# Weight splits, first projections and selection moved into the chunk loop, output projections parked in HBM and done between the heads of a mixture-of-depths block on one core

## The reference

```
# branch 1: gated linear attention, 16 heads of 32, in blocks with a decaying state
q, k, v, u = split(xn @ W_qkvu.T);  q, k = silu(q), silu(k)
o = decayed causal attention(q, k, v) ;  o = u * o * rsqrt(mean(o*o) + 1e-6) ;  y1 = o @ W_out.T
# branch 2: mixture of depths: the router takes 256 of the 2048 tokens
scores = xn @ w_router ;  idx = sort(top_k(scores, 256)) ;  s = xn[idx]
h = rms_norm(s, ln1) ;  q = rope(h@wq + bq) (16 heads of 128), k = rope(h@wk + bk), v = h@wv + bv (8 heads)
x1 = s + causal_softmax_attention(q, k, v) @ wo
processed = x1 + (silu(h2@w_gate) * (h2@w_up)) @ w_down        # h2 = rms_norm(x1, ln2)
y2 = xn ;  y2[idx] = gate*processed + (1-gate)*s               # gate = sigmoid(scores[idx])
output = x + y1 + y2
```

## Time and profile before

| what | value |
|---|---|
| time, median of 3 runs | 641.75 us (632.86 to 777.0) |
| the profiled execution's own time | 638.01 us |
| its span, first to last instruction | 636.3 us |
| busy: TensorE, VectorE, GpSimd, ScalarE | 531.2, 367.6, 280.1, 241.2 us |
| mean granted TensorE clock, as a share of full speed | 0.921 |

### The profile page before, as it was taken

How to read it: one execution, slowest core, us unless ns; L and a number is a source line. 1 busy time by engine, 2 the same in 40 slices (tenths; PEclk the granted TensorE clock), 3 DMA queues, 4 the chain that set the end, 5 groups by cost and what they waited for, 6 DMA issues and landing times.

```text
span 636.3 us, 11375 instructions
## 1 busy us (share of the span) xinstructions
PE 531.2 (83%) x4522; PEld 484.2 (76%) x4522; DVE 367.6 (58%) x651; ACT 241.2 (38%) x418; POOL 280.1 (44%) x183
## 2 busy tenths in 40 slices
PE   3989999999999999999993465846679758599993
PEld 3979998998989989998882444835669757499992
DVE  5886455345534554336676646998897986412231
ACT  7632322222322222235776102343544554434430
POOL 4644544354525453533341635535233233538762
PEclk9999999999999999999996676969869878899998
DMA  8420120110011100020012142242310321225522
GB/s 272 158 35 18 36 33 2 35 35 34 2 35 34 34 7 13 18 83 1 20 56 95 34 148 83 67 132 72 127 67 1 133 67 66 66 81 185 188 78 33
DMA packets 24020, 42.70 MB, mean 67 GB/s; under 512 B 4192, under 2 KB 4192, under 8 KB 23840
## 3 DMA queue, kind: packets, MB, share of 16 engines
q1 hardware_dynamic: 23424, 40.67, 19.9%
q0 software_dynamic: 544, 1.31, 1.1%
HBM read 37.25 MB, written 4.73 MB: 66 GB/s over the span
## 4 chain that ended last, share of the span: by engine, by line
PE 60%; DVE 18%; issue 11%; ACT 6%; POOL 3%; DMA 1%; SPq 0%; DVEq 0%; ACTq 0%; POOLq 0%
PE bank L1115 18%; PE bank L1075 7%; PE bank L1076 7%; PE bank L1077 7%; PE bank L1106 5%; PE bank L1129 4%; DVE staged L829 3%; PE bank L1175 3%; PE bank L1165 3%; DVE rope L826 2%; PE bank L1159 2%; ACT marks L405 2%; DVE rope L824 2%; PE bank L1137 1%; PE bank L1085 1%
## 5 line engine op out<-in xcount | busy, mean ns | idle before, releaser
L1015 POOL TENSOR_TENSOR wlo<-raw,whi 128x2048 fp32r<-128x2048 f32 x24 | 110.9, 4621 | 118.9 <-ACT whi L428 118.9
L1115 PE MATMUL bank<-xTh,Wh 128*128 128x256 f32 x384 | 113.1, 294 | 2.4 <-DVE Wl L620 2.1
L1115 PE MATMUL bank<-xTh,Wl 128*128 128x256 f32 x384 | 109.3, 285 | 0.0
L1115 PE MATMUL bank<-xTl,Wh 128*128 128x256 f32 x384 | 109.2, 284 | 0.0
L1115 PEld LDWEIGHTS bank<-xTh,Wh 128*128 128x128 f32 x384 | 74.3, 194 | 3.4 <-DVE xTl L611 2.5
L1075 PE MATMUL bank<-HTh,whi 128*128 128x256 f32 x224 | 66.4, 297 | 10.4 <-DVE staged L817 6.6
L1115 PEld LDWEIGHTS bank<-xTl,Wh 128*128 128x128 f32 x384 | 74.4, 194 | 0.1
L1115 PEld LDWEIGHTS bank<-xTh,Wl 128*128 128x128 f32 x384 | 74.2, 193 | 0.0
L683 DVE TENSOR_TENSOR A<-bank,DEC 128x512 f32<-128x512 f32 x64 | 39.8, 684 | 52.3 <-PE bank L1129 52.3
L992 POOL TENSOR_TENSOR state<-kv_new,state_dec 128x512 f32<-128x512 f32 x15 | 19.4, 1290 | 110.6 <-DVE kv_new L690 110.6
L1076 PE MATMUL bank<-HTl,whi 128*128 128x256 f32 x224 | 65.9, 294 | 0.0
(11 more groups left out here) (211 smaller groups left out, 1375.6 us busy)
## 6 DMA issues: line engine op xcount, KB each, us to landing
XX<-in_x SPq DMA_DIRECT2D x16, 256.0 KB, 3.0
out<-BASE SPq DMA_DIRECT2D x16, 256.0 KB, 2.7
raw<-in_wq SPq DMA_DIRECT2D x4, 1024.0 KB, 5.1
raw<-in_wo SPq DMA_DIRECT2D x4, 1024.0 KB, 5.5
raw<-in_w_gate SPq DMA_DIRECT2D x4, 1024.0 KB, 4.9
...
```

Source lines behind the costliest of these rows:

```text
L1015: Q.tensor_tensor(wlo[b % 3][:], raw[b % 2][:], whi[b % 3][:].bitcast(f32), ALU.subtract)\
L1115: ins = T.matmul(bank[:, half * GROUP:(half + 1) * GROUP], w[:, k, cols], xt[:, g % 2, k, :], start=m % steps == 0, stop=m % steps == step ...
```

## The change

- **Order of the layer norm.** Normed rows are made two tiles per slot (three ahead of the loop), stored to HBM and loaded again for the transposition from tile 3 on. Router scores are complete after slot 4.
- **Ranking and gather.** The 16 comparisons stand in slots 6 to 9, four in each; choice in slot 10, indices and gather in slot 11, norm, split and transposition of the gathered rows in slot 12. The normed rows themselves are gathered, so the second layer norm of the selected rows is gone.
- **Units in the last chunks.** Slots 14 and 15 hold units 0 to 7 in the places of the projection tiles; their weight blocks are split from slot 13 on, two per slot. Units 8 to 15 stand in head steps 0 to 5, 7 and 8. The output weights become a 25th block (`W0`).
- **Output projections.** `uo` of each chunk is stored to HBM. In head step h (2 to 16) it is loaded back and split, in steps 3 to 16 `project_out(h - 3)` runs, ScalarE moves the result out (`evacuate_out`), VectorE adds the reloaded `x` (`final`), and it is stored. Projections 14 and 15 come behind the heads. Two PSUM banks serve units and output projections in turn.
- **Low halves.** GpSimd writes each low half in four instructions of 128x512. The addition `BASE` on GpSimd is gone; the rms power is taken once for all 16 chunks.
- **Addresses.** Every buffer has a fixed address; blocks lie on top of the first branch's weights, which are free by then.

```diff
-                  "D": tall(w_down)}
-        order = ["K0", "K1", "V0", "Q0", "V1", "Q1", "Q2", "O0", "Q3", "O1", "O2", "O3",
+                  "D": tall(w_down), "W": wide(WoT)}
+        order = ["K0", "Q0", "V0", "Q1", "W0", "K1", "Q2", "V1", "O0", "Q3", "O1", "O2", "O3",
...
-        units = [(k, p) for k in ("K0", "K1", "V0", "Q0", "V1", "Q1", "Q2", "Q3") for p in range(2)]
-        before_heads = 10
...
+        units = [(k, p) for k in ("K0", "Q0", "V0", "Q1", "K1", "Q2", "V1", "Q3") for p in range(2)]
+        in_chunks = 8
+        unit_of_step = {0: 8, 1: 9, 2: 10, 3: 11, 4: 12, 5: 13, 7: 14, 8: 15}
+        PT_AT, OUT_AT, PV_AT, WO_AT, FINAL_AT = 2, 3, 3, 4, 4
...
+        bank_jobs = [("unit", u) for u in range(in_chunks)]
+        for h in range(STEPS):
+            bank_jobs += [("unit", unit_of_step[h])] if h in unit_of_step else []
+            bank_jobs += [("out", h - OUT_AT)] if 0 <= h - OUT_AT < late_outs[0] else []
+        bank_jobs += [("out", N) for N in late_outs]
...
-        rank_in = {(N_TILES - 4, 0): (0, 1), (N_TILES - 4, 1): (2, 3), (N_TILES - 4, 2): (4, 5),
-                   (N_TILES - 3, 0): (6, 7), (N_TILES - 3, 1): (8, 9), (N_TILES - 3, 2): (10, 11),
-                   (N_TILES - 2, 0): (12, 13), (N_TILES - 2, 1): (14, 15)}
-
-        split_after = {2: "Q3", 6: "O1", 7: "O2", 10: "O3", 12: "G0", 15: "U0"}
+        hi_after = {0: "Q2", 1: "V1", 2: "O0", 4: "Q3", 6: "O1", 8: "O2", 9: "O3", 12: "G0", 16: "U0"}
+        load_at = {0: "V1", 1: "O0", 2: "Q3", 3: "O1", 5: "O2", 7: "O3", 9: "G0", 10: "U0", 13: "G1", 17: "U1"}
+
+        def ln_tiles(N):
+            return [M for M in (2 * N + 7, 2 * N + 8) if NX <= M < N_TILES]
+
+        RANK, CHOOSE, INDEX, HIDDEN = 6, 10, 11, 12
+
+        def ranked(N, position):
+            return 4 * (N - RANK) + position if RANK <= N < RANK + N_TILES // 4 else None
...
+            def store_xn(M):
+                sp.wait_ge(xn_ok, M + 1)
+                sp.dma_start(xn_t[M], XN[:, M % NX, :]).then_inc(xn_out[M % NX], 16)
+
+            def load_xn(M):
+
+                sp.wait_ge(xn_out[M % NX], 16 * (M // NX + 1))
+                if M >= NX + 2:
+                    sp.wait_ge(xt_ps, M - 1)
+                sp.dma_start(XA[:, M % 2, :], xn_t[M]).then_inc(xa_in[M % 2], 16)
...
+                if N == N_TILES - 4:
                     load_block(0)
                     load_block(1)
-                    sp.wait_ge(counted, N_TILES)
-                    sp.dma_start(bqk[:, 0:FKV], bk).then_inc(part_in, 16)
-                    sp.dma_start(bqk[:, FKV:], bq).then_inc(part_in, 16)
-                    sp.dma_start(ln12[:, 0, :], ln1).then_inc(part_in, 16)
-                    sp.dma_start(ln12[:, 1, :], ln2).then_inc(part_in, 16)
-                    sp.dma_start(bvb[:], bv.partition_broadcast(P)).then_inc(part_in, 16)
+                if N == N_TILES - 3:
                     load_block(2)
-            store(N_TILES - 2)
-            load_block(3)
-            store(N_TILES - 1)
-            for b in range(4, len(order)):
...
+            for h in range(STEPS):
+                if h in load_at:
+                    load_block(block_of[load_at[h]])
+                if 2 <= h - 1 < N_TILES:
+                    load_uo(h - 1)
+                if 2 <= h - OUT_AT < N_TILES:
+                    load_x_again(h - OUT_AT)
+                if 0 <= h - FINAL_AT < late_outs[0]:
+                    store(h - FINAL_AT)
...
+            def split_uo(N):
+                act.wait_ge(ur_in[N % 2], 16 * (N // 2 + 1)), act.wait_ge(uo_lo, N), act.wait_ge(out_ps, N)
+                S.activation(uoh[:], UR[:, N % 2], ACT.Copy).then_inc(uo_hi, 1)
+
+            def evacuate_out(N):
+
+                act.wait_ge(out_ps, N + 1), act.wait_ge(r_ok, 1), act.wait_ge(gains_ok, 1)
...
+            def final(N):
+
+                dve.wait_ge(evac_ok, N + 1), dve.wait_ge(xr_in[N % 2], 16 * (N // 2 + 1)), dve.wait_ge(gains_ok, 1)
+                V.scalar_tensor_tensor(out=XR[:, N % 2, :], in0=XR[:, N % 2, :], scalar=gain[:, N:N + 1],
+                                       in1=evac[:, N % 2, :], op0=ALU.mult, op1=ALU.add).then_inc(final_ok, 1)
...
             def block_lo(b):
                 pool.wait_ge(fw_hi, b + 1)
-                pool.wait_ge(*last_use(b - 3))
-                Q.tensor_tensor(wlo[b % 3][:], raw[b % 2][:], whi[b % 3][:].bitcast(f32), ALU.subtract)\
-                    .then_inc(fw_lo, 1)
-
-            pool.wait_ge(consts, 1)
-            ln_rstd(0, CH)
-            base(0)
-            base(1)
-            ln_rstd(CH, 1)
+                high, low = halves(b)
+                for k in range(4):
+                    ins = Q.tensor_tensor(low[:, k, :], raw[b % 2][:, k, :], high[:, k, :].bitcast(f32), ALU.subtract)
+                ins.then_inc(fw_lo, 1)
...
+                if N >= N_TILES - 3:
+                    block_lo(2 * (N - (N_TILES - 3)))
...
+            for h in range(STEPS):
+                if 0 <= h - 2 < late_outs[1]:
+                    uo_low(h - 2)
+                if h in hi_after:
+                    block_lo(block_of[hi_after[h]])
+            uo_low(late_outs[1])
             rows_rms(1)
...
             def transposed(M):
 
-                pe.wait_ge(xn_ok, M + 1), pe.wait_ge(masks_ok, 1)
+                pe.wait_ge(masks_ok, 1)
+                if M < NX:
+                    pe.wait_ge(xn_ok, M + 1)
+                    rows = XN[:, M, :]
+                else:
+                    pe.wait_ge(xa_in[M % 2], 16 * ((M - NX) // 2 + 1))
+                    rows = XA[:, M % 2, :]
                 if M >= 2:
...
             def project_out(N):
-                pe.wait_ge(uo_hi, N + 1), pe.wait_ge(uo_lo, N + 1), pe.wait_ge(ms_o_ok, N + 1), pe.wait_ge(w_lo, 1)
+                block_ready(block_of["W0"])
+                pe.wait_ge(uo_hi, N + 1), pe.wait_ge(uo_lo, N + 1)
+                bank_free(("out", N))
                 for k in range(NK):
-                    ins = split_matmuls(out_bank[:], (uoh[:, k, :], uol[:, k, :]), (Woh[:, k, :], Wol[:, k, :]),
+                    ins = split_matmuls(job_bank("out", N)[:], (uoh[:, k, :], uol[:, k, :]), (Woh[:, k, :], Wol[:, k, :]),
                                         k == 0, k == NK - 1)
...
+            def bank_free(job):
+
+                n = bank_jobs.index(job) - 2
+                if n < 0:
+                    pe.wait_ge(proj_sb, NPROJ * G + n + 1)
+                elif bank_jobs[n][0] == "out":
+                    pe.wait_ge(evac_ok, bank_jobs[n][1] + 1)
+                else:
...
-                for u in units_of_step.get(h, ()):
-                    unit(u)
-                if h == PV_AT:
-                    pe.wait_ge(unit_lo, before_heads)
+                if h in unit_of_step:
+                    unit(unit_of_step[h])
+                if h == 0:
+                    rms(N_TILES - 1)
...
+                if 0 <= h - OUT_AT < late_outs[0]:
+                    project_out(h - OUT_AT)
```

1148 lines of the change are left out of this document (602 added, 546 removed).

## The result

The changed kernel takes **607.81 us** (median of 4 runs, 604.61 to 608.34) against 641.87 beside it: a ratio of 0.950, 95% interval 0.940 to 0.961. The ratio is one of means, and leaves out one slow run of the kernel before, of 777.0 us. The change is faster and inside the range (548 to 615), but 26 us above the forecast of 582, outside the forecast's own 560 to 600, and nearer to rival 2's 612. The profiled execution took 607.73 us, its span is 605.7.

What follows compares the result with a forecast made beforehand. TensorE was taken to bound the chunk loop, VectorE and GpSimd in turn the units. Chunks 299 + slots 14 and 15 55 + heads 134 + tail 92.7 = 580.7 us span, 1.7 more gives 582; own range 560 to 600, whole range 548 to 615.

Steps and rivals of the forecast that it cites:

- rival 2: Slots 14, 15 and heads: nothing overlaps, latency adds by a factor of 1.21; 64 and 155 us, 612 in all; chance 0.18.
- Chunks, 299: Slots 0 to 13: thirteen output projections leave TensorE, 35.7 us, and 3 + 1 come in; the stage ends at 299 us.
- issued a slot ahead of their use; hidden: Chunk loop: normed rows go over HBM, 2.7 us out and about as much back, at no cost to the path.
- Slots 14 and 15, 55: Slots 14 and 15 with eight units: VectorE 32 plus GpSimd 32 us, less 9 that may overlap, make 55 us.
- Ends: 36 and 64: Limits for slots 14 and 15: 36 us if TensorE alone bounds, 64 if nothing of VectorE and GpSimd overlaps.
- Heads, 134: Heads: 84 us for steps 0 to 9 plus 50 for steps 10 to 19, sum 134; ends 111 and 155.
- I book no gain for it: Heads: cutting a low half into four lets VectorE in after 1.15 us instead of 4.6, but the total stays the same.
- Four low halves per block instead of one change nothing here: Tail: making each low half in four instructions was to cost or gain nothing there.
- Tail, 92.7: Tail: 88.7 us as before plus 4 us for the later rms power of x1, 92.7 us.
- The two late output projections fit in that gap: Tail: the two late output projections, 5.5 us, fit in the 4 us gap ahead of the transpositions.
- Rival 4: Heads: the ring of two banks makes 16 steps cost 12 us each; 662 us in all, slower than before; chance 0.05.
- steps 10 to 15 at 6 us: Heads, a sign of the forecast: steps 10 to 15 take 6 us each with TensorE busy.

Runs made afterwards that it cites:

- kernels 1: Changed kernel with the store of four router scores asked for behind the reload of normed rows of its slot instead of ahead: 604.10 us, ratio 0.943.
- kernel 2: Changed kernel with the first score stores moved a slot later, behind the reload of their slot, the last two staying: 591.81 us, ratio 0.929.
- kernel 7: Changed kernel, for timing only: GpSimd makes a quarter of the low half for the first seven weight blocks, TensorE reading the high half instead: 595.64 us, ratio 0.932.
- kernel 9: Changed kernel with ScalarE's high halves of blocks 4 and 5 (W0, K1) made earlier in slot 15, block order unchanged: 596.46 us, ratio 0.934.
- kernel 8: Changed kernel with weight block K1 loaded and split ahead of the output weights W0 instead of behind them: 598.81 us, ratio 0.936.
- kernel 6: Changed kernel with two buffer pairs for the split uo and ScalarE's split ahead of the evacuation: 604.48 us, ratio 0.945.
- kernel 5: Changed kernel with four buffers instead of two for the reloaded uo, its load asked for two steps earlier: 604.24 us, ratio 0.941.
- kernel 3: Changed kernel with each low half made by GpSimd in one instruction of 128x2048 again instead of four: 614.41 us, ratio 0.961.
- kernel 4: Changed kernel with rms power ahead of the low half of uo 15 and transpositions ahead of output projection 15: 603.46 us, ratio 0.941.

## Why the prediction was right, and where it was not

- **Right: what bounded the kernel, and where the gain comes from.** TensorE's 65 us half idle turned into units; slots fell from 20.4 to 17.65 us, the 2.75 us of the earlier trace rows. The ranking is absorbed: slots 6 to 9 are 17.65 to 17.9 us long.
- **Chunks, 299 against 308.0: the step that failed is "issued a slot ahead of their use; hidden".** I priced the reload by the landing of a large transfer and did not ask what else was in flight. The store of scores in its neighbourhood held the reload back, 6.7 us ahead of tile 3 (kernels 1 and 2). The other part of the start, 4.3 us of wait, is the way over HBM itself (the reload asked for at 33.8 us was seen 3.8 us later in kernel 2), which I had left out with "The start (0 to 41.2) I leave". The stores cost 5.6 us more in slots 1 and 3, where no reload was waited for; what the engines stood for there is open. With the stores moved, slots 0 to 13 take 249.3 us, 8.5 less than I had counted (257.8): 3.9 us of small waits that TensorE had in the loop before the change went too; the other 4.6 I have not traced.
- **Slots 14 and 15, 55 against 59.3: right in size, wrong in cause.** I had VectorE and GpSimd fully in turn. GpSimd was idle for 13 us waiting for ScalarE, an engine that my sum did not hold at all. Taking three quarters of GpSimd's work away gave 12 us (kernel 7); another place for two instructions of ScalarE gave 11 (kernel 9), and another order of the blocks 9 (kernel 8), with the same work for all engines. That VectorE and GpSimd slow each other there is real (kernel 7), but not what set the end. "Ends: 36 and 64" covered it, by luck more than by reason.
- **Heads, 134 against 138.3,** counted from the start of unit 8. To step 10 it took 82.8 us (forecast 84), from there to the end 55.5 (50). TensorE's pace in the steps of 5 to 9 with a unit is the sum of rows to 0.1 us. What I lacked in the last ten steps was the single pair of buffers of the split uo: with two pairs steps 11 to 19 fell by 4.3 us, the ten steps by only 1.9, since step 10 grew (kernel 6). A reload of uo took 5.6 us to landing, not the 2.7 to 3.0 of the earlier trace rows that I priced it by; four buffers won 0 to 1 us in the profile, so it was all but hidden (kernel 5).
- **Low halves in four: "I book no gain for it" was wrong**, by 9 us in the heads (kernel 3). The argument that VectorE's next instruction meets the next piece holds for the engines' sum; what counts is the engine that TensorE waits for. "Four low halves per block instead of one change nothing here", said of the tail, was wrong too, by 1 to 3 us the other way.
- **Tail, 92.7 against 100.1.** I charged the rms power 4 us; it cost 6.9, since the transpositions also stood behind projection 15, which itself waited 4.1 us and ran at half clock. "The two late output projections fit in that gap" is the sentence that failed; with another order 4.2 us of it come back (kernel 4). That is 2.9 of the 7.4 us I was short; the other 4.5 lie behind the first gate matmul (84.8 us to the end, 80.3 before), where kernels with the same code took 81.4 to 85.7. At most 3.5 of them are the four pieces (kernel 3); the rest has no cause shown.
- **The rivals.** Rival 2's time (612) was near, its mechanism was not: a uniform factor on all waits, where the runs show places that can each be taken away. The range held because it had been stretched up to this rival, and not because its mechanism was seen. Rival 4's ring of two banks showed once, 2.4 us in step 4, where a unit waited for the bias of the one before it; from step 5 on the steps with a unit and a projection took 8.6 to 8.7 us, without it. Of the signs I had named, the wait for K1's low half ahead of unit 8 came, and no wait of TensorE behind slot 14 names a DMA; "steps 10 to 15 at 6 us" did not hold for steps 10 and 11 (7.8 and 7.2) and 14 (7.3).
